# First loop of a decoder kernel: queries and keys projected once, unpadded, and their split parts laid into every fourth row by transfers

## What is computed

```python
q = (x @ Wq).reshape(B, N, H, Dh)
k = (x @ Wk).reshape(B, N, H, Dh)
v = (x @ Wv).reshape(B, N, H, Dh)
scores = jnp.einsum('bqhd,bkhd->bhqk', q, k) * Dh ** (-0.5)
attn = jax.nn.softmax(scores, axis=-1)
std_out = jnp.einsum('bhqk,bkhd->bqhd', attn, v).reshape(B, N, D)
# splat branch: influences of 64 positions on the tokens, gather, encode, transform, decode, flow, gate
out = (STD_RATIO * std_out + SPLAT_RATIO * flow) @ Wo
```

## Time and profile before

| | us |
|---|---|
| median of three runs | 1932.77 |
| lowest and highest | 1927.73, 1934.17 |
| span of the profiled execution | 1930.1 |
| first and last reduction of straight scores in it (L1021) | 16.56, 429.47 |
| busy: PE | 1723.1 |
| busy: DVE | 1374.7 |
| busy: ACT | 1189.4 |
| busy: POOL | 1037.7 |

### The profile page before, as it was taken

How to read it: one execution, slowest core, us unless ns; L and a number is a source line. 1 busy time by engine, 2 the same in 40 slices (tenths; PEclk the granted TensorE clock), 3 DMA queues, 4 the chain that set the end, 5 groups by cost and what they waited for, 6 DMA issues and landing times. The chain is left out here.

```text
span 1930.1 us, 43925 instructions
## 1 busy us (share of the span) xinstructions
PE 1723.1 (89%) x15676; PEld 1312.7 (68%) x15676; DVE 1374.7 (71%) x4606; ACT 1189.4 (62%) x2858; POOL 1037.7 (54%) x1590
## 2 busy tenths in 40 slices
PE   7999999988899999999999999999879999589930
PEld 5666666656777777777777777776656667479930
DVE  6788888873767788888888888897657876611127
ACT  3566666642688777778778777776315776244412
POOL 3566676663245565655666565666421442175375
PEclk8999999999999999999999999999988999689975
DMA  2000000000200000000000000000000000345322
GB/s 56 9 13 15 15 16 15 12 5 27 75 1 2 1 2 7 8 7 8 7 8 7 6 3 7 6 4 6 6 27 15 27 21 16 99 70 75 60 64 83
DMA packets 57824, 44.03 MB, mean 23 GB/s; under 512 B 13952, under 2 KB 50186, under 8 KB 57482
## 3 DMA queue, kind: packets, MB, share of 16 engines
q1 hardware_dynamic: 52330, 30.11, 5.4%
q0 software_dynamic: 4608, 9.45, 3.3%
q10 hardware_dynamic: 672, 1.67, 0.2%
HBM read 26.52 MB, written 13.63 MB: 21 GB/s over the span
## 5 line engine op out<-in xcount | busy, mean ns | idle before, releaser
L2281 POOL TENSOR_SCALAR probs<-probs,rsums 128x128 f32<-128x128 f32 (+1 forms) x512 | 208.7, 426 | 307.6 <-DVE rsums L2178 306.7
L1061 POOL TENSOR_SCALAR at_least<-magnitudes,candidates 128x512 bf16<-128x512 f32 x128 | 198.2, 1564 | 151.3 <-DVE candidates L950 151.3
L2162 DVE CUSTOM_DVE_ANT_0 probs<-dist,pq,nmin 128x128 f32<-128x128 f32 (+1 forms) x512 | 181.2, 409 | 76.0 <-PE pq L1622 75.6
L1902 ACT ACTIVATE probs<-probs,low 128x130 f32<-128x130 f32 (+1 forms) x512 | 227.7, 460 | 6.3 <-DVE low L2162 6.2
L1021 DVE TENSOR_REDUCE negmax<-ps_scores 128x4 f32<-128x1024 f32 x128 | 156.2, 1221 | 53.6 <-PE ps_scores L629 51.9
L812 ACT ACTIVATE pT<-ps_scoresT 128x1024 f32<-128x1024 f32 x128 | 131.1, 1024 | 61.8 <-PE ps_scoresT L638 55.2
L2172 DVE COPY pT<-pq 128x384 f32<-128x384 f32 x256 | 129.8, 547 | 4.1 <-PE pq L1637 4.1
L1815 ACT ACTIVATE qn<-pq 128x512 f32<-128x512 f32 x128 | 77.2, 603 | 81.4 <-PE pq L1479 79.8
L1622 PE MATMUL pq<-k1T,q1T 64*128 64x128 f32 (+1 forms) x1024 | 119.3, 351 | 0.4 <-ACT k1T L1830 0.3
L3302 POOL DMA_INDIRECT m_x<-token_rows,m_idx_put x80 | 75.8, 947 | 80.7 <-DVE m_idx_put L3232 33.3
L3254 DVE COPY m_y<-pm 128x256 f32<-128x256 f32 x40 | 17.0, 424 | 140.6 <-PE pm L3140 140.6
(11 more groups left out here) (543 smaller groups left out, 5293.4 us busy)
## 6 DMA issues: line engine op xcount, KB each, us to landing
expert_answers<-m_y SPq DMA_DIRECT2D x40, 128.0 KB, 2.0
m_w<-in_L_ffn_moe_w_dram SPq DMA_DIRECT2D x16, 256.0 KB, 5.9
x<-in_x_dram SPq DMA_DIRECT2D x16, 128.0 KB, 2.2
x_mid<-x SPq DMA_DIRECT2D x16, 128.0 KB, 1.8
y<-x_mid SPq DMA_DIRECT2D x16, 128.0 KB, 2.2
x_mid<-y SPq DMA_DIRECT2D x16, 128.0 KB, 1.8
cx<-x_mid SPq DMA_DIRECT2D x8, 256.0 KB, 3.0
token_rows<-c_hn SPq DMA_DIRECT2D x8, 256.0 KB, 2.0
```

The costliest lines, as they stand in the source:

```text
L1061: pool.tensor_scalar(at_least[:, a, :], mags[:, 512 * (a // 2):512 * (a // 2) + 512], cf[:, a:a + 1], None, ALU.is_ge).then_inc(mask_ready ...
L1902: ins = act.activation(probs[:, a, keys_nulls(i, w)], probs[:, a, keys_nulls(i, w)], ACT.Exp, bias=low[:, a, i:i + 1], scale=-1.0, accum_o ...
L2162: ins = dve.tensor_tensor_reduce(probs[:, a + t, keys(i, w)], dist[:, (1 - t) * P:N], ps[:, t * P:t * P + w], slopes[h], nmin[u][:, t, h:h ...
L2281: ins = pool.tensor_scalar(probs[:, a + t, keys(i, w)], probs[:, a + t, keys(i, w)], rsums[:, a + t, i:i + 1], 1.0, ALU.mult, ALU.mult)
```

## The change

- The weights are no longer padded: one product of 128 columns for q and one for k (`wq_turned`, `wk_turned`, columns ordered by j, d, group), both into one bank. `project_qk` runs once a batch, at offset −9, which is step 7.
- `round_qk` is one ACT instruction for q and k together, into the blocks 0 and 3 of `parts`; `rest_qk` is one DVE instruction, which writes the low parts into the blocks 1 and 2, then waits for its own end and releases the bank.
- A new stage `place_qk` on SP at offset −6 (step 2) waits for the low parts, and from batch 3 on for `pT` of the batch three before (whose buffer `qkT` is taken over); it issues three transfers of 256 KB (each lays 128 partitions x 2 blocks into every fourth row of `qkT`), and a fourth of 128 KB, which writes zeros into the query rows in which the maxima come later. The key rows there are set to one by POOL before the loop; the first `place_qk` waits for that.
- Contractions run over 32 rows. The first scores of a batch wait for the placed parts instead of the banks of k. The maxima are placed with one transfer instead of four.
- The setup on DVE loses two memsets and four of six copies of the weights.

```diff
-        rounded = two("qk_rounded", [P, 2 * N], F32R)
-        qT = sets(3, "qT", [P, GROUPS, N], F32R)
-        kT = sets(3, "kT", [P, GROUPS, N], F32R)
+        parts = two("qk_parts", [P, 4, N], F32R)
+        no_rows = sb("no_max_rows", [P, N])
+        qkT = sets(3, "qkT", [P, GROUPS, 2, N], F32R)
...
-            (-11, "load"), (33, "store"), (-8, "q0"), (-6, "k0"), (-4, "q1"), (-2, "k1"), (5, "gather"),
+            (-11, "load"), (33, "store"), (-9, "qk"), (5, "gather"),
...
-            (-8, "split_q0"), (-6, "split_k0"), (-4, "split_q1"), (-2, "split_k1"), (8, "turn_rows"),
+            (-9, "rest_qk"), (8, "turn_rows"), (-6, "place_qk"),
...
+            def project_qk(u):
+                ring.wait_read(pe, "xT", u)
...
+                ps = ring.open(pe, "qk", u, held=0.95)
+                for i, w in enumerate((wq, wk)):
+                    mm = pe.matmul(ps[:, i * N:(i + 1) * N], w[:].rearrange("p j d g -> p (j d g)"), xT[u][:],
+                                   start=True, stop=True)
+                mm.then_inc(ring.filled("qk", u), 1)
...
+                    if p == 0:
+                        pe.wait_ge(*qk_placed[u % 2].at(PLACED * (u // 2 + 1)))
...
+            def round_qk(u):
+                ps = ring.wait(act, "qk", u)
+                if u >= 2:
+                    act.wait_ge(*qk_placed[u % 2].at(PLACED * (u // 2)))
+                act.activation(parts[u][:, 0:4:3, :], ps[:].rearrange("p (i n) -> p i n", i=2), ACT.Copy)\
+                    .then_inc(rounded_ready.sem, 1)
...
+            def rest_qk(u):
+                ps = ring.bank("qk", u)
+                dve.wait_ge(*rounded_ready.at(u + 1))
+                dve.tensor_tensor(parts[u][:, 1:3, :], ps[:].rearrange("p (i n) -> p i n", i=2),
+                                  parts[u][:, 0:4:3, :].bitcast(F32), ALU.subtract).then_inc(rest_ready.sem, 1)
+                dve.wait_ge(*rest_ready.at(u + 1))
+                dve.sem_inc(ring.read("qk", u), 1)
...
+            pool.memset(no_rows[:], 0.0)
+            for i in range(3):
+                ins = pool.memset(qkT[i][:, :, 1, :].bitcast(F32), 1.0)
+            ins.then_inc(pool_keys, 1)
...
+                def place_qk(u):
+                    if u == 0:
+                        sp_eng.wait_ge(pool_keys, 1)
+                    sp_eng.wait_ge(*rest_ready.at(u + 1))
+                    if u >= 3:
+                        sp_eng.wait_ge(*pT_ready.at(PAIRS * (u - 2)))
+                    for part, blocks in enumerate((slice(0, 4, 3), slice(0, 3, 2), slice(1, 4, 2))):
+                        sp_eng.dma_start(qkT[u][part:P:4].bitcast(F32), parts[u][:, blocks, :].bitcast(F32))\
+                            .then_inc(qk_placed[u % 2].sem, 16)
+                    sp_eng.dma_start(qkT[u][3:P:4, :, 0, :].bitcast(F32), no_rows[:]).then_inc(qk_placed[u % 2].sem, 16)
```

More of the change, by code:

```diff
@@ L385, in loop_1 @@
         pT_ready = Counted(sem("probsT_ready"))
-        rounded_ready = Counted(sem("rounded_ready"))
+        rounded_ready = Counted(sem("qk_rounded_ready"))
+        rest_ready = Counted(sem("qk_rest_ready"))
+        qk_placed = [Counted(sem(f"qk{i}_placed")) for i in range(2)]
         on_ready = Counted(sem("o_normal_ready"))
@@ L432, in loop_1 @@
         PIECE = NS // 2 // 4
+        PLACED = 16 * 4
         stages = [
```

86 lines of the change are left out of this document (21 added, 65 removed).

## The result

The changed kernel takes 1961.07 us in the median of four executions (1947.76 to 1969.83), against 1933.47 for the kernel before. The ratio is 1.0132, with a 95% interval from 1.0083 to 1.0181: slower, 16.6 us above the 1944.5 that was forecast, and outside the range of 1921 to 1955. The profiled execution is the quickest of the four, 1947.8 us; the other three, at 1958.0 to 1969.8, have a lower mean clock of TensorE (0.924 to 0.930 against 0.936). What the profile shows of the clock is thus the mildest case of the four.

A forecast was written before the change was run, and what follows sets the result against it. PE, busy 89%, was not taken as sole bound: the reduction's chain and POOL's masks limit steps. 1930.1 + 0.2 (steps and start) + 11.5 (clock) = 1941.8, plus 2.7 to the median: 1944.5 us; range 1921 to 1955.

The forecast's parts named there:

- What bounds the kernel: Steady loop: not PE alone; the chain scores, reduction, scores (no step under 1.85 us) and POOL's masks limit the gain.
- Even batch: Steady even batches: steps 2, 4, 6 and 0 save 0.7, 0.6, 1.2 and 0.2 us, step 7 grows 1.3; sum −1.4.
- Odd batch: Steady odd batches: steps 1 and 2 −0.1 us, step 4 +0.1, steps 6 and 0 nothing, step 7 +1.1; sum +1.1.
- The start: Before the steady loop: x of batch 1 queues behind the placement, first scores about 4 us later; net +3.5 us, ends +1.5 and +12.
- my 6 us for the bytes: At the start: the time taken for moving the 896 KB of the placement, between bounds of 4.6 plus about 1.5 and 15 us.
- The steady transfers: Steady loop: placement has 18 us, from step 2 to step 0, and the load of x 11 us; hidden in both batches.
- The clock: TensorE falls to half clock in all seven even batches (5 x 1.5 us) and every second odd one (4 x 1.0): +11.5 us.
- Its own upper end, 30: Upper end of the clock term: a fall in every batch and place named, some 20 x 1.5 = 30 us.
- x coming late: Rival in the steady loop: load of x behind the placing takes over 11 us, or the clock falls everywhere named; 1960 us, 13%.
- five of seven even batches passed at full clock: Kernel before: argument for the rival that the clock holds and the steady loop wins and loses nothing; 1933 us, 25%.
- The new fills of `qkT` by POOL: At the start: POOL's four memsets lie beside the load of x and cost nothing unless POOL's end after 9.7.

The follow-up runs named there:

- e5_qk_step0: The changed kernel with projection, rounding and subtraction of q and k one step later, in step 0: 1932.7 us, ratio 1.0001 to the kernel before.
- the two runs from opposite sides: `e3_wide_back`, which puts wide products back into the changed kernel (1941.1 us), and `e8_before_thin`, which takes them from the kernel before (1949.6 us).
- e3_wide_back: The changed kernel with twelve wide PE instructions a batch put back in steps 2, 4 and 6, into an unread bank: 1941.1 us, ratio 1.0043.
- e8_before_thin: The kernel before, with three of its four projections replaced by short bf16 products from batch 2 on: 1949.6 us, ratio 1.0102.
- e10_step0_odd_filled: The changed kernel with projection in step 0, early load of batch 1, and wide filler in steps 2, 4, 6 of odd batches only: ratio 0.9970.
- e4_load_early: The changed kernel with x and context of batch 1 sent for ahead of the placing transfers: 1954.8 us, ratio 1.0111.
- e9_step0_filled: The changed kernel with projection in step 0, early load of batch 1, wide filler in odd steps 2, 4, 6 and even step 6: ratio 0.9961.
- e7_combo: The changed kernel with early load, values off the encoding's bank, wide filler in odd steps 2, 4, 6 and even step 6: 1927.3 us, ratio 0.9982.
- e11_bf16_filler: As `e9_step0_filled`, but each filler is nine bf16 products instead of four f32 instructions: ratio 0.9982 to the kernel before.

## Why the prediction was wrong

- **What bounds the kernel:** right. PE's lost instructions are not won as such; the reduction's chain sets steps 2 and 6 of the even batches, at the 1.85 us named.
- **Even batch:** right, step by step; the forecast was −1.4, measured −1.26. Step 7 grew by 1.31 where 1.3 was reckoned: the projection takes 1.06 (1.0) and the wait for x transposed 0.2 (0.3).
- **Odd batch:** forecast +1.1, measured +0.61. Steps 1 and 2 together are 4.66 as reckoned, step 4 grew by 0.13 (0.1), step 7 by 1.02 (1.1; the terms written out there add up to 5.03 and not 5.1, which is +1.03), with the wait for L785's counterpart where it was named. The miss is step 0, which I gave nothing: 0.34 less, because q0 had stood in front of the maxima there; with the projection back in step 0 (`e5_qk_step0`) it is 4.17 again.
- **The start:** first scores 3.84 us later, forecast about 4; by batch 2 it was 2.0 behind, forecast 3.5. I had the order of the queue right and its length wrong. x of batch 1 is sent for at 12.64 instead of 4.05: SP waits 5.8 us for the low parts, until 9.86 (9.7 in the forecast), and then issues four transfers in 2.8 us; it doesn't wait for their landing, which is over an estimated 4.5 us after the first issue (the fourth goes out at 11.96 and lands in 2.4). By my 6 us for the bytes x would have gone out near 15.7, 3 us later than it did, so that the scores came at the time forecast is luck.
- **The steady transfers:** hidden, right.
- **The clock:** this is the step that failed: the term of +11.5 us for the falls was mis-sized. The mechanism was named (q1 and the others are the wide work that held the clock) and the two runs from opposite sides bear it out. The size was wrong three times over. *How often:* I counted one fall in each of seven even batches, five more than before, and one in every second odd batch; there were enough for 73 us at half clock against 6. *Where:* I looked only at step 5, where the clock had fallen in batches 4 and 14; from batch 4 to 13 it never fell there, more than half of the time at half clock came in step 7, where the work is PE's alone, and a fall there cost 2.6 to 3.1 us in an even batch instead of 1.5. The trace of the kernel before had shown that place too, in step 7 of batch 3 and step 0 of batch 4 (the two stretches below this list: length first, clock third from the end), at a cost of 1.4 us; the forecast passed over it. *Their spread:* I took the median 2.7 us above the profiled execution, as in the kernel before; but three of four executions have a lower clock than the profiled one, and lie 10 to 22 us above it. The term was +11.5 and measured +22 in batches 2 to 13 of the profile; the median lies 15.1 us above the span instead of 2.7. Its own upper end, 30, was in the text, and stood among the rivals at 13%, in one line with x coming late; it was what happened.

```profile
113.61:118.28 4.67, 3.88 (x37) 2.00 (x36) 3.92 (x11) 2.87 (x9) 4.67 (x4) 0.86 0.01 4
118.28:122.16 3.88, 3.88 (x59) 3.20 (x55) 2.82 (x7) 2.14 (x4) 2.53 (x5) 0.73 0.00 0
```

So the miss adds up. Of the 16.6 us, 12.4 are the spread between span and median, and 4.2 the span itself (1946.0 against 1941.8): the clock made 10.5 more in batches 2 to 13 than its whole term, the full-clock steps of batches 2 to 13 gave 2.1 more than forecast (−3.9 against −1.8), and start and ends 4.1 more, 2.9 of them in the two loops whose code is the same. That these offset a part of the clock's miss is chance.

The argument that set this too low was that five of seven even batches passed at full clock. That was read as a margin. I now read two falls in seven batches of the same code as a loop at the edge: the change took 2.9 us of wide work out of a batch of some 25 us, and the clock then fell in every even batch from 4 to 12, in another step than the one that I watched.

The Trainium skill, "TensorE: Matmul & The Clock Gate", Part 1, says that activity releases the throttle. `e3_wide_back` agrees (idle filler brought 0.89 to 0.99). PE was busy for 88% of the stretch in the changed kernel and for 91% in `e8_before_thin`, against 94% in the kernel before; but it was busy for 96% in `e10_step0_odd_filled`, at a clock of 0.90. The share of busy time over the stretch, as the profile counts it, doesn't tell on which side a loop stands.

## What to carry to other kernels

Before work is taken off TensorE in a loop that shows even one or two falls of its granted clock, price the loop at half clock in its longest TensorE-only step, in every iteration; then look where a product to no use can stand behind the scores, while another engine holds the chain, at little cost (0 to 0.7 us each here). Put work that is moved into a step that has slack (here step 0, where the maxima are waited for), not into the fullest one: two numbers in the table took the ratio from 1.0132 to 1.0001 (on another chip, each against the kernel before). Filler in front of a step's first product cost 70 to 100% of its length in every step, some 30 us here. None of the kernels with the change gained more than 0.4% on the kernel before.

## What the runs showed of the hardware

**Two DVE instructions of 1.6 us took 4.7.** In `e4_load_early` the first projection waited 2.67 us for the weights, which DVE copies at the start. DVE and POOL there, timeline:

```profile
3.21 4.74 DVE L833 TENSOR_SCALAR wq_turned<-wq_raw 128x128 f32<-128x128 f32 x1 [1.73 <-DMA wq_raw<-in_L_attn_Wq_dram]
3.35 4.71 DVE L835 COPY wk_turned<-wk_raw 128x128 f32<-128x128 f32 x1
...
4.63 0.95 POOL L1031 MEMSET v<- 128x1024 f32 x1
```

The same rows of the changed kernel:

```profile
3.23 1.60 DVE L833 TENSOR_SCALAR wq_turned<-wq_raw 128x128 f32<-128x128 f32 x1 [1.75 <-DMA wq_raw<-in_L_attn_Wq_dram]
3.37 1.57 DVE L835 COPY wk_turned<-wk_raw 128x128 f32<-128x128 f32 x1
...
4.63 1.20 POOL L1031 MEMSET v<- 128x1024 f32 x1
```

POOL sets memory from 1.71 to 8.2 without a break. In the changed kernel DVE's two instructions end at 4.83 and 4.94, and POOL's instruction at 4.63 takes 0.25 us longer; in `e4_load_early` they end at 7.95 and 8.06, and it is POOL's instruction at 7.76 that takes 0.24 us longer (0.44 against 0.20). DVE's start differs by 0.02 us and its end by 3.1. The quick form is the rarer one: of the changed kernel and the ten kernels made from it, seven profiles show 4.5 to 5.0 us (`e9_step0_filled` 4.72), three 1.6 to 1.9 (`e7_combo` 1.57), and `e11_bf16_filler` 0.75. Each time DVE ends some 0.2 us behind the start of an instruction of POOL that is 0.25 us longer than its like. It looks as if DVE gets in between two of POOL's instructions, now at one boundary and now several later; no run tried to take POOL's work away. The Trainium skill, "SBUF — State Buffer", section "SBUF: two separate sides", describes the pair of ports that DVE and GpSimd share as an exclusive lock held for a whole instruction. The rows agree with that in so far as DVE ends just behind a boundary; that it can stay shut out over several instructions in a row, 4.7 against 1.6 us, they show beyond it. The new fills of `qkT` by POOL, which the prediction called free, are thus not free in most executions: in the slow form the first projection starts at 7.9 to 8.2 us instead of 6.1 to 6.4.

**Transfers cost their issuer.** Three placing transfers and the zeroing take SP's queue 2.8 us (9.86 to 12.64), 0.6 to 0.7 each; 256 KB land in 2.6 us in the median, against 2.1 for the 128 KB of the earlier trace rows.
